# A pipeline of one attention stage stretched by two rounds, with a sixth slot

## What is computed

```
neg_inner = einsum('bhie,bhje->bhij', tq, tk) - einsum('bhid,bhjd->bhij', sq, sk)
dist   = arccosh(maximum(neg_inner, 1.0 + 1e-07))
scores = where(causal, -dist ** 2 / sqrt(D), -inf)
attn   = softmax(scores, axis=-1) * spike_mask
y      = einsum('bhij,bhjd->bhid', attn, v)
```

## Time and profile before

| | |
|---|---|
| median of 3 runs | 4466.02 us (4456.5 to 4469.49) |
| the profiled execution | 4458.36 us, of which 4456.6 us are its span |
| span by engine | PE 79%, PEld 44%, DVE 51%, ACT 37%, POOL 21% |
| mean granted TensorE clock | 0.900 |
| stage Da in the four passes, from its first instruction | 476.3, 1445.5, 2414.9 and 3380.9 us |

### The profile page before, as it was taken

How to read it: one execution, slowest core, us unless ns; L and a number is a source line. 1 busy time by engine, 2 the same in 40 slices (tenths; PEclk the granted TensorE clock), 3 DMA queues, 4 the chain that set the end, 5 groups by cost and what they waited for, 6 DMA issues and landing times. The chain is left out here.

```text
span 4456.6 us, 58459 instructions
## 1 busy us (share of the span) xinstructions
PE 3514.0 (79%) x22310; PEld 1971.3 (44%) x22310; DVE 2255.7 (51%) x4289; ACT 1635.7 (37%) x2451; POOL 919.0 (21%) x993
## 2 busy tenths in 40 slices
PE   3887778898887688888886688988876788955995
PEld 2423453436324355245334445255234534345884
DVE  2465766552465855634556765624657665530111
ACT  0343643242443733332344732423445532411221
POOL 0101542001202722011104611011115421021002
PEclk9988789998998799999897799999887899977998
DMA  4111102100203011101112012011111021024453
GB/s 77 36 54 71 15 2 78 47 20 20 76 14 85 1 40 43 44 28 48 43 30 67 1 41 67 19 38 37 54 71 15 1 75 51 20 98 155 165 173 125
DMA packets 242705, 238.79 MB, mean 54 GB/s; under 512 B 111870, under 2 KB 207852, under 8 KB 239980
## 3 DMA queue, kind: packets, MB, share of 16 engines
q1 hardware_dynamic: 234224, 217.91, 16.4%
q0 software_dynamic: 3072, 8.39, 0.6%
q10 hardware_dynamic: 5116, 8.58, 0.6%
HBM read 166.15 MB, written 68.68 MB: 53 GB/s over the span
## 5 line engine op out<-in xcount | busy, mean ns | idle before, releaser
L842 ACT ACTIVATE prob<-psum 128x1024 f32<-128x1024 f32 x384 | 372.2, 1021 | 548.4 <-PE psum L762 548.4
L1173 ACT ACTIVATE prob<-psum 128x1024 f32<-128x1024 f32 (+3 forms) x384 | 331.2, 914 | 435.0 <-PE psum L1093 435.0
L883 DVE TENSOR_REDUCE scr<-psum 128x1 f32<-128x512 f32 x576 | 371.4, 685 | 204.8 <-PE psum L749 200.6
L1211 DVE TENSOR_REDUCE stats<-psum 128x1 f32<-128x512 f32 (+3 forms) x576 | 334.0, 620 | 162.1 <-PE psum L1081 157.4
L380 PE MATMUL psum<-ident 128*128 128x128 f32 x2464 | 303.6, 284 | 16.6 <-PEq L69 8.9
L380 PEld LDWEIGHTS psum<-ident 128*128 128x128 f32 x2464 | 297.2, 200 | 28.1 <-issue 27.2
L1093 PE MATMUL psum<-stack 32*128 32x512 f32 (+3 forms) x1536 | 210.2, 618 | 64.8 <-ACT prob L1173 34.8
L759 PE MATMUL psum<-stack 32*128 32x512 f32 x1536 | 226.4, 659 | 31.1 <-DVE xo L873 24.7
L790 PE MATMUL psum<-prob,ones_f 128*32 128x512 f32 x1536 | 204.8, 601 | 0.0
L1108 PE MATMUL psum<-prob,vbig 128*32 128x512 f32 (+3 forms) x1536 | 188.9, 565 | 4.3 <-ACT prob L1173 4.3
L2469 PE MATMUL psum<-xgT,ew 128*128 128x256 f32 x736 | 167.7, 387 | 18.0 <-DVE xgT L2515 18.0
(11 more groups left out here) (429 smaller groups left out, 6729.2 us busy)
## 6 DMA issues: line engine op xcount, KB each, us to landing
ew<-in_L_ffn_W SPq DMA_DIRECT2D x46, 1024.0 KB, 7.5
stack<-q_terms SPq DMA_DIRECT2D x144, 128.0 KB, 2.4
w_mlp<-in_L_xattn_a_li_w SPq DMA_DIRECT2D x16, 1024.0 KB, 6.3
q_terms<-parts SPq DMA_DIRECT2D x96, 128.0 KB, 2.1
stack<-k_terms SPq DMA_DIRECT2D x72, 128.0 KB, 2.7
w_mlp<-k_terms SPq DMA_DIRECT2D x36, 256.0 KB, 4.5
w_mlp<-a_terms SPq DMA_DIRECT2D x36, 256.0 KB, 4.7
a_keys<-stack SPq DMA_DIRECT2D x4, 2048.0 KB, 7.2
```

The source lines that it names most:

```text
L842: act.activation(prob[:, i % 4, :, :], psum[:, 2 * p:2 * p + 2, :], ACT.Exp, scale=scale).then_inc(exped, 1)
L883: dve.tensor_reduce(found[:, c:c + 1], ring(i), AX.X, ALU.max).then_inc(freed, 1)
L1173: act.activation(prob[:, i % 4, :, q0:T], psum[:, 2 * p:2 * p + 2, q0:T], ACT.Exp, scale=scale).then_inc(exped, 1)
L1211: dve.tensor_reduce(found[:, c:c + 1], ring(i)[:, 0:keys_of(t)], AX.X, ALU.max).then_inc(freed, 1)
```

## The change

Two slots are added to what the five-slot ring had: the sixth slot of `near` is `xT`, that of `weight` is `cnT`; both tensors are free in this stage. And the rounds of the steps move. In round i:

| step | engine | before | now |
|---|---|---|---|
| above_one, times_itself | DVE, POOL | i + 1 | i + 1 |
| log_of_square, root, add_root | ACT, POOL | i | i |
| distance | ACT | i - 1 | i - 1 |
| square | DVE | i - 2 | i - 2 |
| exponentiate, cut | ACT, POOL | i - 2 | i - 3 |
| turn | PE | i - 3 | i - 4 |
| copy_second | ACT | i - 3 | i - 5 |
| copy_first | DVE | i - 3, at the round's end | i - 5, at its start |
| weigh | PE | i - 4 | i - 6 |
| gather, lift | PE, DVE | i - 5 | i - 7 |
| spread, invert | PE, DVE | i - 6 | i - 8 |
| divide | DVE | i - 7 | i - 9 |

```
-    SLOTS = 5
+    SLOTS = 6
-    near.append(e.xh[:, :, :].rearrange("p t n -> p (t n)"))
+    near += [v[:, :, :].rearrange("p t n -> p (t n)") for v in (e.xh, e.xT)]
...
 tensor:
-                if 0 <= i - 3 < NU:
-                    turn(i - 3)
                 if 0 <= i - 4 < NU:
-                    weigh(i - 4)
+                    turn(i - 4)
+                if 0 <= i - 6 < NU:
+                    weigh(i - 6)
...
 vector:
+                if 0 <= i - 5 < NU:
+                    copy_first(i - 5)
                 if i + 1 < NU:
                     above_one(i + 1)
                     times_itself(i + 1)
                 if 0 <= i - 2 < NU:
                     square(i - 2)
-                if 0 <= i - 3 < NU:
-                    copy_first(i - 3)
...
 scalar:
-                if 0 <= i - 2 < NU:
-                    exponentiate(i - 2)
                 if 0 <= i - 3 < NU:
-                    copy_second(i - 3)
+                    exponentiate(i - 3)
+                if 0 <= i - 5 < NU:
+                    copy_second(i - 5)
...
 gpsimd:
-                if 0 <= i - 2 < NU:
-                    cut(i - 2)
+                if 0 <= i - 3 < NU:
+                    cut(i - 3)
```

More of the change, by code:

```diff
@@ L1937, in hyperbolic_attention @@
     two_banks = [sum(u[4] * (u[2] + 1) > 4 for u in units[:i + 1]) for i in range(NU)]
-    SLOTS = 5
+    SLOTS = 6
     near = [r[:, i * 1024:(i + 1) * 1024] for r in (e.vbig[:, VW:2 * VW], e.parts2[:, :].bitcast(F32)) for i in range(2)]
-    near.append(e.xh[:, :, :].rearrange("p t n -> p (t n)"))
-    weight = [e.prob[:, i, :, :].rearrange("p a n -> p (a n)") for i in range(4)] + [xo[:, :, :].rearrange("p t n -> p (t n)")]
+    near += [v[:, :, :].rearrange("p t n -> p (t n)") for v in (e.xh, e.xT)]
+    weight = [e.prob[:, i, :, :].rearrange("p a n -> p (a n)") for i in range(4)] + [v[:, :, :].rearrange("p t n -> p (t n)") for v in (xo, e.cnT)]
     by_pool = [i % 3 != 0 for i in range(NU)]
@@ L2008, in _ @@
                 score(1)
-            for i in range(NU + 7):
+            for i in range(NU + 9):
                 if i + 1 < NU and i + 1 in last_unit and units[i + 1][0] + 1 < len(quads):
                     score(units[i + 1][0] + 1)
-                if 0 <= i - 3 < NU:
-                    turn(i - 3)
                 if 0 <= i - 4 < NU:
-                    weigh(i - 4)
[L2016 to L2019, removed]
+                    turn(i - 4)
+                if 0 <= i - 6 < NU:
+                    weigh(i - 6)
+                if i - 7 in ends:
+                    gather(ends.index(i - 7))
+                if i - 8 in ends:
+                    e.spread_inverses(pe, ends.index(i - 8), inverted, spread_in)
         @block.vector
@@ L2063, in _ @@
             times_itself(0)
-            for i in range(NU + 8):
+            for i in range(NU + 10):
+                if 0 <= i - 5 < NU:
+                    copy_first(i - 5)
                 if i + 1 < NU:
@@ L2069, in _ @@
                     square(i - 2)
-                if 0 <= i - 3 < NU:
-                    copy_first(i - 3)
[L2072 to L2075, removed]
-                if i - 7 in ends:
-                    e.divide(dve, then, ends.index(i - 7), spread_in, divided)
+                if i - 7 in ends:
+                    lift(ends.index(i - 7))
+                if i - 8 in ends:
+                    e.invert(dve, ends.index(i - 8), gathered, inverted)
+                if i - 9 in ends:
+                    e.divide(dve, then, ends.index(i - 9), spread_in, divided)
         @block.scalar
@@ L2118, in copy_second @@
                 act.copy(turned_w[i % 2][:, T:n], psum[:, 5, 0:n - T]).then_inc(copied_b, 1)
-            for i in range(NU + 3):
+            for i in range(NU + 5):
                 if i < NU:
@@ L2157, in _ @@
             times_itself(0)
-            for i in range(NU + 2):
+            for i in range(NU + 3):
                 if i + 1 < NU:
```

## The result

The changed kernel takes 4546.16 us (median of 4 runs, 4531.21 to 4548.83), the kernel before 4467.57 beside it (4 runs, 4456.5 to 4469.49): ratio 1.0174, 95% interval 1.0146 to 1.0203. The forecast was 4511, so 45 us of loss, and 78.6 were measured. The profiled spans are 4547.1 and 4456.6, 90.5 apart. The stage Da, from the start of its first instruction to the end of the last division, took 146.2, 143.0, 143.8 and 143.8 us in the four passes, 576.8 together; now 164.5, 164.5, 164.4 and 164.5, 657.9. So 81.1 of the 90.5 us are here. The other 9.4 lie spread over stages that the change does not touch, and I do not explain them. The spans are further apart than the medians because the profiled execution of before was 9.2 us under its median and that of the changed kernel 2.7 us above.

The account below looks back on a forecast made before the run. The prediction took waits between engines to bound stage Da. Per pass, 6.9 steady state - 1.5 start + 5.8 end = 11.2 us, 45 in four; 4466 + 45 = 4511 us, range 4485 to 4545 (chance 0.53).

Parts of the forecast that it names:

- What bounds the stage: Stage Da is held by waits between engines: 33.2 us a group of six units, busiest engine working 27.3.
- What is removed: ScalarE's wait for squares, 21.4 us, mostly goes; valued at 1.5 us a pass, at the stage's start.
- The steady state: Units 5 to 23, three groups: 35.5 us a group, 2.3 more than before, 6.9 us a pass.
- (a): VectorE's first copy waits for value products now issued right behind its unit's transposes; 0.92 us a unit on average.
- (b): TensorE's transposes wait for ScalarE's second copy, now in the same round, losing a 3.2 us head start.
- normalising: Lift and division ahead of VectorE's copy, 0.6 us each, counted as hidden where VectorE waits anyway.
- the long loop: Two-round loop through TensorE, VectorE, GpSimd and ScalarE: 10.70 us on average, 32.1 a group, before squares add 3.4.
- The end: After the last square root, two more units are transposed, weighed and copied in a row, 2.9 us each: +5.8 a pass.
- The sum: Stage Da: 6.9 - 1.5 + 5.8 = 11.2 us more a pass, 45 in four passes.
- Rival 1: Faster: the removed waits were the bound and the new loop never closes; -17 us in all, 4449; chance 0.10.
- Rival 2: No measurable change: GpSimd and VectorE's two-input operations set the period, 33.1 of 33.2 us; 4466 to 4483; chance 0.17.
- Rival 3: Slower: all squares on the path, TensorE at the low clock; 40.0 us a group, 107 in all, 4573; chance 0.20.

Follow-up runs that it names:

- i: Changed kernel with VectorE's clamp moved ahead of its first copy in each round: 4489.69 us, ratio 1.0076.
- c: Changed kernel with ScalarE's second copy and the value products each one round earlier, so neither new wait is left: 4450.57 us, ratio 0.9967.
- a: Changed kernel with only ScalarE's second copy one round earlier, undoing wait (b): 4509.43 us, ratio 1.0102.
- e: Kernel before with only the value products, gathering, normalising and division one round later, adding wait (a): 4521.19 us, ratio 1.0137.
- h: Run c's kernel with VectorE's eight multiplications of a pass done by ScalarE as squares: 4423.69 us, ratio 0.9915.
- j: Kernel before with VectorE's eight multiplications of a pass done by ScalarE as squares: 4437.36 us, ratio 0.9935.
- k: Changed kernel with VectorE's eight multiplications of a pass done by ScalarE as squares: 4518.99 us, ratio 1.0123.
- d: Changed kernel with GpSimd's add_root(i) moved ahead of times_itself(i + 1) in each round: 4582.76 us, ratio 1.0262.

## Why the prediction was right in direction and short in size

- **What bounds the stage.** Waits and not a full engine, as said: the loops were there, and cutting one link (i) changed the time without changing any instruction.
- **What is removed.** Its value was put at 1.5 us a pass, in the start. The third pass reached the root of unit 5 after 27.83 us, before after 27.97, so 0.1. In c, where the new waits don't cover it, all that moves is worth 7.7 us of stage in four passes, 1.9 a pass. So little was right, but not by my reason alone: the squares take 7 to 10 us more a pass beside GpSimd.
- **The steady state: the step that failed.** Forecast 2.3 us a group and 6.9 a pass. From the root of unit 5 to that of unit 23 the third pass took 98.9 us before and 112.3 now: 13.4 more, 4.5 a group, and the group shown took 39.2 instead of 35.5. The waits (a) and (b) were named rightly; the sum that gave them their price was short. It put TensorE's scores at nothing, and they take 1.3 to 2.6 us in four rounds of six and stand ahead of the transposes: 0.86 us of the 12.86. It took ScalarE's stretch from one round, 3.39 us, where the lap shown has 4.09. It counted normalising as hidden, but the copy at 2540.09 starts right behind the copy of the inverses, and the score at 2542.10 right behind the products that spread them (L1259, 2.08 us from 2540.23). How the missing 6.5 us divide among these, the squares and the next point is not shown.
- **The circle that was not summed.** I wrote that the copy "now waits for transposes plus products", and then summed that only into the long loop; the loop of one round, with which my own text begins, was never summed again. It is copy, clamp, score, transposes, products and handovers. In the lap shown it closes at 6.29 us, and a and e price wait (a) by itself at 47 and 52 us of stage. With the prediction's own durations, the 1.28 us from score to transposes in the earlier trace rows and a handover of 0.1 it would have come to 0.71 + 0.94 + 1.28 + 1.27 + 0.92 + 0.1 = 5.2 us, an estimate from its rows and under the 5.35 of the long loop. So summing it would not have mended the number by itself. Its terms were too small as well: the score took 1.71 us there, the transposes 1.89 until the products started.
- **Durations at the lower clock.** I took 0.92 us for products and 1.27 for transposes. Over units 6 to 17 of the third pass they took 1.20 and 1.38 on average, 0.39 us a unit more. With the clock granted at 0.65 in this stage, rows like these stand where I had put the middle or the high level; what lowered the clock was not tried by itself:

```profile
2504.80 1.94 PE L1984 MATMUL psum<-ident,xo 128*128 128x128 f32 x8 [0.77 <-ACT stack L2118]
...
2519.43 1.92 PE L1997 MATMUL psum<-stack,vbig 128*32 128x128 f32 x16
```

- **The end.** Forecast +5.8 a pass. From the last root, 2597.98, to the start of the last division, 2621.62, now pass 23.64 us, 16.3 before: +7.3. The two units in a row are there, the first of them with transposes at the low clock, not the high one:

```profile
2597.98 0.61 ACT L2094 ACTIVATE cnT<-cnT 128x512 f32<-128x512 f32 x1
...
2600.53 1.94 PE L1984 MATMUL psum<-ident,prob 128*128 128x128 f32 x8 [0.91 <-DVE stack L2056]
...
2621.62 0.69 DVE L1268 TENSOR_TENSOR yT<-ob,psum 128x512 f32<-128x512 f32 x1 [1.25 <-PE psum L1259]
```

- **The sum.** -0.1 + 13.4 + 7.3 = 20.6 us in the third pass, where 11.2 stood. Of the missing 9.4, 6.5 are the steady state, 1.5 the end and 1.4 the start. Four passes: 81 in the stage.
- **The rivals.** Rival 1 is refuted with the waits in place: the new loop does close. For the rest of the change c shows a gain of a third of a per cent; its 4450.57 us are too near that run's line of 4449 to decide more. Rival 2, that the shared ports of VectorE and GpSimd set the period in both kernels, fell: its loop would hide (b), and (a) and (b) cost 47 and 35 us. VectorE's load is still worth something in all three kernels, 27 us in h, j and k. Rival 3 named 40.0 us a group, nearer to 39.2 than the 35.5 of the forecast, and it claimed all results above 4545: the 4546.16 measured lie 1 us on its side of the forecast's own range, though inside the wider one. Its low clock was seen, in the products more than in the transposes for which it named it (0.28 and 0.11 us a unit), and its squares stood on the path before some copies. So rival 3 had more of the mechanism than the chance of 0.20 gave it, and its 4573 was too much.

## What to carry to other kernels

In a pipeline over several engines, write down after every shift each circle of waits with the number of rounds over which it closes, buffers that are reused included, and sum all of them, short ones first, with all that stands in program order between their steps. A shift that only puts a producer and the reuse of its buffer into one round can cost more (here 47 and 35 us of stage) than the removed wait was worth (7.7). When a circle is closed, look for the cheapest link to cut: here one swap of two independent operations on VectorE (i) gave back half of the stage's loss, 40.5 of 81.1 us. Sum the circles again after the swap: another one, on GpSimd (d), closed a new circle and cost 37 us more.

## What the runs showed of the hardware

VectorE's squares, 57.4 us in the third pass of the kernel before, took 64.0 in the changed kernel and 75.6 in i, with the same 128 instructions. Two squares of one unit, 384 columns each, with GpSimd's sum beside the second:

```profile
2523.47 0.55 DVE L2048 CUSTOM_DVE_ANT_0 parts<-parts 128x384 f32<-128x384 f32 x1
...
2523.89 2.36 POOL L2148 TENSOR_TENSOR xT<-xT,cnT 128x1024 f32<-128x1024 f32 x1 [1.53 <-ACT cnT L2094]
...
2523.95 2.72 DVE L2048 CUSTOM_DVE_ANT_0 parts<-parts 128x384 f32<-128x384 f32 x1
```

It is not only operations with two inputs. VectorE's copy of the inverses (L1253), from SBUF to SBUF, took 0.43 us in the median of 48 and 2.29 at most. In the kernel before, its maximum was 0.71. One of the long ones ran beside a sum on GpSimd:

```profile
2537.09 2.79 POOL L2148 TENSOR_TENSOR vbig<-vbig,prob 128x1024 f32<-128x1024 f32 x1
...
2537.89 2.28 DVE L1253 COPY scr<-inverse 128x512 f32<-128x512 f32 x1
```

The Trainium skill's page "SBUF — State Buffer", section "Who interferes with whom", names copies that can enter a mode of two ports among those that contend with GpSimd; the trace agrees in that this copy took 2.28 us beside GpSimd and 0.43 in the median, but no row shows its mode. The same page says that the loser waits for the whole instruction, and the square of 2.72 us agrees with that: it ends 0.42 us after GpSimd's sum.
